# Second spread's 200 scatters in the first mixer: behind other gathered batches, in larger groups, none in the last forward pass

## What is computed

```python
xn = _layernorm(x, axis=-1)
# graph part: y[dst] += edge_weight * xn[src], then two projections with batch norms
msgs = edge_vals[:, None] * x[edge_src]
agg = jax.ops.segment_sum(msgs, edge_dst, num_segments=N)
# mixer part, DEPTH = 4
for i in range(DEPTH):
    h = _layernorm(x, ln1_g[i], ln1_b[i])
    x = x + _linear_attn(h, Wq[i], Wk[i], Wv[i], Wo[i], bo[i])
    h = _layernorm(x, ln2_g[i], ln2_b[i])
    x = x + (jax.nn.gelu(h @ W1[i] + b1[i], approximate=False) @ W2[i] + b2[i])
```

## Time and profile before

| | us |
|---|---|
| median of 3 runs | 6076.75 |
| profiled execution | 6084.95 |
| its span | 6083.2 |
| PE busy | 5215.5 (86%) |
| DVE busy | 3406.0 (56%) |
| ACT busy | 2920.7 (48%) |
| POOL busy | 3377.0 (56%) |

### The profile page before, as it was taken

How to read it: one execution, slowest core, us unless ns; L and a number is a source line. 1 busy time by engine, 2 the same in 40 slices (tenths; PEclk the granted TensorE clock), 3 DMA queues, 4 the chain that set the end, 5 groups by cost and what they waited for, 6 DMA issues and landing times. The chain is left out here.

```text
span 6083.2 us, 86153 instructions
## 1 busy us (share of the span) xinstructions
PE 5215.5 (86%) x25560; PEld 4420.9 (73%) x25560; DVE 3406.0 (56%) x8766; ACT 2920.7 (48%) x7115; POOL 3377.0 (56%) x3345
## 2 busy tenths in 40 slices
PE   2288999999989999888887799999678888887799
PEld 1167888788878888777776688888356666665688
DVE  8875777444445555433333555554667777776541
ACT  5354555455645555444443333333355555564444
POOL 0266766666356666666663655554337777777000
PEclk9999999999999999989888899999789999998899
DMA  3122112213233333333354322221324444445401
GB/s 106 28 65 68 47 47 54 55 47 89 82 99 102 104 104 104 109 95 95 95 93 98 103 59 56 56 59 36 94 75 109 112 108 113 111 111 95 96 28 34
DMA packets 378325, 493.02 MB, mean 81 GB/s; under 512 B 97680, under 2 KB 315784, under 8 KB 375432
## 3 DMA queue, kind: packets, MB, share of 16 engines
q0 software_dynamic: 135008, 236.92, 16.5%
q1 hardware_dynamic: 242856, 250.61, 14.2%
HBM read 385.22 MB, written 102.04 MB: 80 GB/s over the span
## 5 line engine op out<-in xcount | busy, mean ns | idle before, releaser
L1837 POOL DMA_INDIRECT messages_g<-h_rows,messages_idx x880 | 924.2, 1050 | 440.0 <-issue 266.0
L238 POOL DMA_INDIRECT sorted_dst<-edges_record,edges_place x784 | 800.2, 1021 | 632.8 <-POOLq L88 242.4
L238 POOL DMA_INDIRECT sorted_src<-edges_record,edges_place x784 | 764.2, 975 | 672.5 <-issue 214.1
L286 POOL DMA_INDIRECT edges_g<-xn_rows,edges_idx x880 | 864.1, 982 | 455.0 <-issue 253.4
L1120 PE MATMUL mixer_y_ps<-mixer_w,mixer_g 128*125 128x256 f32 x3200 | 772.2, 396 | 68.7 <-ACT mixer_g L1266 68.7
L1109 PE MATMUL mixer_f_ps<-mixer_f_out,mixer_w 128*128 128x250 f32 x3200 | 754.7, 379 | 8.0 <-issue 3.6
L1120 PEld LDWEIGHTS mixer_y_ps<-mixer_w,mixer_g 128*125 128x125 f32 x3200 | 621.3, 197 | 173.1 <-ACT mixer_g L1266 77.2
L1109 PEld LDWEIGHTS mixer_f_ps<-mixer_f_out,mixer_w 128*128 128x128 f32 x3200 | 604.3, 193 | 77.7 <-issue 6.1
L2006 PE MATMUL forward_s_ps<-messages_g,messages_one 128*128 128x257 f32 x1760 | 476.0, 417 | 124.3 <-DVE messages_one L1917 120.3
L2006 PEld LDWEIGHTS forward_s_ps<-messages_g,messages_one 128*128 128x128 f32 x1760 | 341.3, 203 | 204.1 <-DVE messages_one L1917 153.1
L305 DVE TENSOR_TENSOR edges_acc<-edges_acc,mixer_s_ps 128x257 f32 x440 | 186.1, 423 | 497.8 <-PE mixer_s_ps L324 429.6
(11 more groups left out here) (514 smaller groups left out, 10203.7 us busy)
## 6 DMA issues: line engine op xcount, KB each, us to landing
mixer_q<-qT SPq DMA_DIRECT2D x100, 250.0 KB
mix_rows<-mixer_rows SPq DMA_DIRECT2D x100, 250.0 KB
qT<-mixer_qT SPq DMA_DIRECT2D x75, 250.0 KB, 3.5
mixer_rows<-mix_rows SPq DMA_DIRECT2D x75, 250.0 KB
edges_g<-xn_rows,edges_idx POOLq DMA_INDIRECT x880, 3.6
messages_g<-h_rows,messages_idx POOLq DMA_INDIRECT x880
sorted_dst<-edges_record,edges_place POOLq DMA_INDIRECT x784
sorted_src<-edges_record,edges_place POOLq DMA_INDIRECT x784
```

The lines of the kernel that those rows point to most:

```text
L238: self.nc.gpsimd.indirect_dma_start(self.orders[s][0], bass.IndirectOffsetOnAxis(self.place[s][:, j:j + 1], 0), self.record[s][:, j, :], N ...
L286: self.nc.gpsimd.indirect_dma_start(self.g[n % GR][:, j, 0:D], None, self.table_d, bass.IndirectOffsetOnAxis(self.idx[:, t:t + 1], 0)).the ...
L1837: self.nc.gpsimd.indirect_dma_start(self.g[n % GR][:, j, :], None, self.table_d, bass.IndirectOffsetOnAxis(self.idx[:, t:t + 1], 0)).then_inc(
```

## The change

The 200 scatters of the second spread keep their order and number, and stand elsewhere in GpSimd's queue: 64 behind batch 4, in eight runs of eight, each run waiting until all earlier ones have landed; then eight behind each third batch, 9, 12, ... 57 (17 times). Behind batches 58 to 109 there are none. `pool_spread_eights` may now start at record 0, and `pool_spread_landed` waits for both counters.

```diff
-BESIDE = 4
...
             if (j - j0) % (2 * FOUR) == 0:
                 for b in range(2):
-                    pool.wait_ge(self.spread[b], 16 * FOUR * ((four + 1 - b) // 2))
+                    if four > b:
+                        pool.wait_ge(self.spread[b], 16 * FOUR * ((four + 1 - b) // 2))
...
     def pool_spread_landed(self, pool, j1):
-        four = (j1 - 1) // FOUR
-        pool.wait_ge(self.spread[four % 2], 16 * FOUR * (four // 2 + 1))
+        fours = j1 // FOUR
+        for b in range(2):
+            pool.wait_ge(self.spread[b], 16 * FOUR * ((fours + 1 - b) // 2))
...
-    in_forward = [n for n in range(GR, NB - GR) if n % 2]
-    behind = {n: BESIDE * k for k, n in enumerate(in_forward)}
-    start = BESIDE * len(in_forward)
+    share_of = {n: 2 * FOUR for n in range(9, 60, 3)}
+    share_of[GR - 1] = 16 * FOUR
+    until = dict(zip(sorted(share_of), itertools.accumulate(share_of[n] for n in sorted(share_of))))
+    start = max(until.values())
...
-                if n in behind:
+                if n in share_of:
                     pool.wait_ge(edges.landed[n % GR], 16 * 2 * PB * (n // GR + 1))
-                    edges.pool_spread_second(pool, behind[n], behind[n] + BESIDE)
-                    edges.pool_spread_landed(pool, behind[n] + BESIDE)
+                    edges.pool_spread_eights(pool, until[n] - share_of[n], until[n])
+                    edges.pool_spread_landed(pool, until[n])
```

## The result

The changed kernel takes 5933.71 us (median; 5925.69 to 5940.29 in four runs) against 6075.38 for the kernel before beside it: a ratio of 0.9768, 95% interval 0.9748 to 0.9787, so 2.3% faster. The prediction was 5926 us, its range 5895 to 5985. The profiled execution took 5940.29 us, 5938.5 of it span, where the one before took 6084.95 and 6083.2.

The account below looks back on a forecast made before the run. GpSimd, a third of its time on scatters, was taken to pace the fourth forward pass. 21 slots x 7.19 = 151.0 us off 6084.95 gives 5933.9 profiled, about 5926 us median, other terms about 0; range 5895 to 5985.

Parts of the forecast that it names:

- GpSimd paces the last pass, by its scatters: Fourth forward pass: GpSimd's gathers and scatters set the 29.99 us slot; without scatters 22.8, gaining 7.19 a slot, 151.0 us.
- The buffers do not become the next bound: Fourth pass: with five buffers, batches are gathered in time (25.0 against 28.5 us), so the slot is TensorE's 22.8 us.
- The clock comes back: Fourth pass: TensorE, no longer waiting, returns from a mean clock of 0.90 to near 1.00 and holds 22.8 us slots.
- the rival in which it does not: Fourth pass: TensorE takes 26.4 us a slot, so only 76 us are gained, 6001 us; chance 0.07.
- The 22 us of the empty batches stay: Mixer's last three slots, batches 104 to 109 without edges: 22.0 us excess stays; bounds: all goes, or as much again.
- Batch 5 lands just in time: Behind batch 4: 64 scatters take 107.5 us, batch 5 lands at 1628.8, scaled at 1628.35 before; cost 0 to 1 us.
- Groups of eight cost nothing in the third pass: Third pass: three batches and a group take 45.5 us, 30.33 for two, against TensorE's 30.34; taken as 0.
- Nothing behind the mixer changes: Later stages: scatters of message layer and experts start at record 200 as before, so nothing moves there.
- The sum: Whole kernel: profiled execution 6084.95 less 151.0 is 5933.9 us; median about 5926 us, 2.5% less.
- Late in passes two and three: Rival: the run of 64 and the groups of eight delay gathers, 23 us lost, 5949 us; chance 0.09.
- Empty batches harmless: Rival: batches 104 to 109 start earlier against their use and stop hurting, 22 us less, 5904 us; chance 0.06.
- Dense gathers slow the DMA engines: Rival, fourth pass: gathers without pauses make every slot 37.3 us, 132 us slower, 6209 us; chance 0.04.

Follow-up runs that it names:

- experiment 3: Kernel before, groups of four only behind odd batches 5 to 59, 88 other scatters in the experts' stage: ratios 0.9954, 0.9800, 0.9857, whole time left open.
- experiment 5: Changed kernel with 32 scatters behind batch 4, and eight groups of four behind odd batches 61 to 75: 7308.47 against 7321.29 us, no verdict.
- Experiment 1: Changed kernel with blank slots naming a row for each lane instead of row 0 for all: 5898.73 us, ratio to the kernel before 0.9706.
- experiment 2: Changed kernel with 96 scatters behind batch 4 instead of 64, and 13 groups of eight instead of 17: 5979.34 us, ratio 0.9842.

## Why the prediction was right

- **GpSimd paces the last pass, by its scatters.** Right. Clearing it gave 22.94 us a slot for the 22.8 of the forecast, and the price of a group comes back as 6.6 and 7.6 us (119.4 and 137.2 over 18 slots, experiment 3) and 8.1 (experiment 5). The gain of the 18 even slots is 126.9 where 18 x 7.19 = 129.4 was reckoned.
- **The buffers do not become the next bound.** Right: ScalarE's wait for gathers is 0, not the "under 25 us" left at the end. GpSimd waits 2.7 and 0.6 us in each slot for a buffer.
- **The clock comes back.** Right: 1.00 over 390 us, and the rival in which it does not is out. The tail shows the reverse, 0.50 from 3035 to 3045 us, while TensorE has nothing to do. Both agree with the Trainium skill ("TensorE: Matmul & The Clock Gate", Part 1), by which the default is the throttled clock and activity releases it.
- **The 22 us of the empty batches stay.** Of the right kind and too small: this is the term that was mis-sized. They grew to 29.5 us, so the last three slots gained 13.65 instead of 21.6. What was reckoned is whether the empty batches themselves arrive in time (six "just fit"); what stops TensorE is a load beside them. That load had 18.7 us between issue and use instead of 25.2, which is the reason that the prediction gave for its own upper bound and did not put into the sum, and it took 46.1 us instead of 38.3, which it did not foresee. Experiment 1 shows that the repeated row is the cause of the whole excess; the 7.7 us stay open.
- **Batch 5 lands just in time.** Right, with 3.7 us to spare. From the end of batch 4's last gather to the first of batch 5 are 104.3 us; 107.5 were reckoned.
- **Groups of eight cost nothing in the third pass.** Right: from batch 6 to 66 it takes 920.2 us before and 920.8 after.
- **Nothing behind the mixer changes.** Right for the sum; that the later stages would have no room for more was not looked at, since the change asks nothing of them.
- **The sum.** 5933.9 us for the profiled execution, 5940.29 measured. The tail is 7.9 short, the even slots 2.5, and 4.2 us up to batch 66 were not expected. 3.1 of these lie ahead of the change and are luck, so the sum is nearer to the result than its terms are.
- **The rivals.** Late in passes two and three: not seen, but experiment 2 shows that it would be real from some two more scatters on. Empty batches harmless: the opposite, they cost more. Dense gathers slow the DMA engines: not so with distinct rows (0.46 for 125 GB/s over 390 us), and so with one row. The Trainium skill ("DMA: Bandwidth & Descriptors", section "Queues, rings and completion order") has each DMA engine take turns between its queues; at a load of 0.46 nothing of that shows in TensorE's slot, and a wait for `mixer_q` shows only where the engines are full.

## What to carry to other kernels

Find the engine that paces one stage by its own slot (issue by issue) and move its side work to where it stands idle anyway; measure that gap and fill it only so far, because the 32 scatters beyond it cost their whole time here. Before sending work to a later stage, look when that engine ends there against the stage's end. And where slots of a gather are left blank, give each its own row: here a padding index that all lanes share cost three times as much per byte as rows of data, and 30 us of the mixer.

## What the runs showed of the hardware

- Gathers in which 128 lanes read one and the same row of 1 KB hold the DMA engines about three times as long per byte: 100% for 87 GB/s, against 46% for 125 GB/s with rows of their own. The same gathers with distinct rows went at 52% for 157 GB/s.
- Such gathers hold up other queues too: a 250 KB load issued in 3.30 us beside them kept TensorE waiting until 46.1 us after its issue, and the issue of the next one on SyncE's queue took 22.13 us; with distinct rows both were issued in 0.6 us and TensorE waited for neither.
- A scatter of 128 records costs GpSimd 1.57 to 1.60 us in long runs of eight, waits for landing among it.
